# Score products that run 24 ahead of the transposed ones instead of 32, the first rows of maxima sent before the weights, and the first batch's key rows sent by ScalarE

## What is computed

```python
mod = silu(c) @ wmod                      # six vectors per batch: sa, ca, ga, sb, cb, gb
h = layernorm(x) * (1 + ca) + sa          # x is (4, 512, 256)
q, k, v = h @ wq.T, h @ wk.T, h @ wv.T    # 16 heads of 16
p = softmax(q @ k.T)                      # no scaling of the scores
x = x + ga' * ((p @ v) @ wo.T)            # ga', gb': sign kept, size at least 0.25
h = layernorm(x) * (1 + cb) + sb
r = softmax(h @ gate.T); top 4 of 32 experts, weights normalised
y = sigmoid(h @ sg) * shared(h) + sum over 4 experts of w_e * (silu(h@g_e) * (h@u_e)) @ d_e
x = x + gb' * y
```

## Time and profile before

| what | value |
|---|---|
| median of 3 runs | 648.5 us (648.0 to 648.52) |
| the profiled execution | 650.28 us |
| its span, first to last instruction | 648.5 us |
| TensorE busy | 584.2 us, 90% of the span |
| VectorE busy | 378.5 us, 58% |
| ScalarE busy | 261.3 us, 40% |
| GpSimd busy | 200.2 us, 31% |
| mean granted TensorE clock | 0.965 |

### The profile page before, as it was taken

The page is one execution under the profiler, slowest core; times in us unless marked ns, Lnnn a source line. Parts: engine busy times, 40 slices in busy tenths (PEclk is TensorE's granted clock), DMA queues, the critical chain, the costliest instruction groups (busy, mean ns, idle before and its releaser), DMA issues.

```text
span 648.5 us, 10653 instructions
## 1 busy us (share of the span) xinstructions
PE 584.2 (90%) x3118; PEld 320.4 (49%) x3119; DVE 378.5 (58%) x874; ACT 261.3 (40%) x523; POOL 200.2 (31%) x268
## 2 busy tenths in 40 slices
PE   4999999899998999989999998999889999999271
PEld 3453242234433344332433464565778889889251
DVE  6285757766769667696773665653534444444083
ACT  3214445654666646554456512001234344344100
POOL 6100000000000830007300480362256666666442
PEclk9957999999999999999999999999999999999797
DMA  6142161101401223012100127922455565552393
GB/s 210 37 129 86 34 198 28 30 2 41 83 8 28 90 85 82 6 30 83 50 1 2 41 83 322 266 101 66 121 147 147 156 170 155 163 161 53 107 410 131
DMA packets 41958, 67.17 MB, mean 104 GB/s; under 512 B 9099, under 2 KB 31764, under 8 KB 41564
## 3 DMA queue, kind: packets, MB, share of 16 engines
q1 hardware_dynamic: 29824, 45.62, 24.7%
q0 software_dynamic: 7680, 16.87, 7.5%
q10 hardware_dynamic: 4416, 4.20, 1.9%
HBM read 38.93 MB, written 27.51 MB: 102 GB/s over the span
## 4 chain that ended last, share of the span: by engine, by line
PE 73%; DVE 9%; DMA 5%; issue 4%; ACT 3%; POOL 3%; SPq 1%; POOLq 0%; ACTq 0%; DVEq 0%
PE ps L791 21%; PE ps L804 9%; PE ps L1017 8%; PE ps L1038 6%; PE ps L885 5%; PE ps L743 5%; PE ps L879 4%; DVE max_q L1121 3%; PE ps L1006 3%; PE ps L763 2%; DMA up_sb<-results 2%; PE ps L751 2%; PE ps L817 2%; POOL dispatched L457 2%; ACT probs L625 2%
## 5 line engine op out<-in xcount | busy, mean ns | idle before, releaser
L1121 DVE TENSOR_REDUCE max_q<-ps 128x1 f32<-128x512 f32 x256 | 163.2, 683 | 91.9 <-PE ps L763 90.8
L625 ACT ACTIVATE probs<-ps 128x512 f32<-128x512 f32 x256 | 138.2, 595 | 106.8 <-PE ps L791 106.7
L791 PE MATMUL ps<-q_rows,k_rows 32*128 32x512 f32 x512 | 153.7, 647 | 11.4 <-ACT probs L625 10.3
L763 PE MATMUL ps<-k_rows,q_rows 31*128 31x512 f32 x512 | 155.0, 687 | 0.3 <-DMA k_rows<-qk_raw 0.3
L475 POOL DMA_INDIRECT results<-y_sb,dest x96 | 94.5, 984 | 72.3 <-ACT y_sb L676 37.2
L791 PEld LDWEIGHTS ps<-q_rows,k_rows 32*128 32x128 f32 x512 | 49.0, 185 | 92.6 <-ACT probs L625 56.3
L1017 PE MATMUL ps<-up_sb,oT 128*128 x384 | 70.9, 328 | 1.3 <-issue 1.2
L804 PE MATMUL ps<-probs,v_ext 128*32 128x512 f32 x512 | 68.2, 605 | 0.0
L1017 PEld LDWEIGHTS ps<-up_sb,oT 128*128 128x128 f32 x384 | 61.3, 190 | 2.3 <-issue 2.2
L442 POOL TENSOR_TENSOR rstd<-veps,mhalf 128x4 f32<-128x4 f32 x4 | 4.1, 1037 | 167.4 <-DVE veps L1190 167.3
L763 PEld LDWEIGHTS ps<-k_rows,q_rows 31*128 31x128 f32 x512 | 48.7, 194 | 10.3 <-DVE max_q L1121 6.3
(11 more groups left out here) (172 smaller groups left out, 689.2 us busy)
## 6 DMA issues: line engine op xcount, KB each, us to landing
xe<-dispatched SPq DMA_DIRECT2D x96, 129.0 KB, 2.2
up_sb<-results SPq DMA_DIRECT2D x16, 512.0 KB, 8.5
up_sb<-in_up SPq DMA_DIRECT2D x2, 3072.0 KB, 14.8
dispatched<-pad_rows SPq DMA_DIRECT2D x33, 129.0 KB, 4.8
down_sb<-in_down SPq DMA_DIRECT2D x1, 3072.0 KB, 31.7
x<-in_x ACTq DMA_DIRECT2D x4, 512.0 KB, 5.2
q_rows<-qk_raw SPq DMA_DIRECT2D x64, 32.0 KB, 2.0
k_rows<-qk_raw SPq DMA_DIRECT2D x64, 32.0 KB, 2.0
```

What stands on the lines that cost most here:

```text
L625: act.activation(probs[:, u % 8, :], ps[:, st_bank(t.b, g, u), :], ACT.Exp).then_inc(exp_done, 1)
L763: pe.matmul(ps[:, banks[u % len(banks)], :], q_rows[32 * i:32 * i + ONE, b % 2, g, qt * P:(qt + 1) * P], k_rows[32 * i:32 * i + ONE, b % 2 ...
L791: pe.matmul(ps[:, st_bank(b, g, n), :], k_rows[32 * i:32 * i + 32, b % 2, g, kt * P:(kt + 1) * P], q_rows[32 * i:32 * i + 32, b % 2, g, :] ...
L1121: dve.tensor_reduce(max_q[:, g % 2, qt, i:i + 1], ps[:, banks[(16 * g + n) % len(banks)], :], AXX, ALU.max).then_inc(max_done, 1)
```

## The change

The lead is a number now, `LAG = 24`, and every place that had 32 or "two groups" goes by it. The lead-in does 8 score products of group 1 instead of 16. `turn_max` and `negate_max` move from u = 1 to u = 9, since the group's last maximum now exists eight steps later, and `ORDER` follows with the same entries in another order. In the last batch the steps by four begin at (2,8) instead of (2,0). In the lead-in the row of maxima is sent ahead of the loads of weights, and the keys' 16 DMAs are issued by ScalarE, between its copies. `place_rows` of later batches issues the same DMAs as before.

The number, the order of bank uses (first lines; the three other groups of the table move their `MAX` entry in the same way), the banks, and what is ahead of a step:

```diff
+LAG = 24
...
     ORDER = (
-        ("MAX0", "att"), ("TP0", "pre"), ("TP1", "pre"), ("QK0", "pre"), ("SG0@0", "fill"),
+        ("TP0", "pre"), ("TP1", "pre"), ("QK0", "pre"), ("SG0@0", "fill"), ("MAX0", "att"),
...
         def st_bank(b, g, n):
 
-            if b == B - 1 and g >= 2:
-                return (ST + SC)[(16 * (g - 2) + n) % 5]
+            alone = 16 * g + n - (16 * NG - LAG)
+            if b == B - 1 and alone >= 0:
+                return (ST + SC)[alone % 5]
             return ST[n % 2]
+
+        def ahead(b, g, n):
+
+            u = 16 * NG * b + 16 * g + n + LAG
+            return (u // (16 * NG), u // 16 % NG, u % 16) if u < 16 * NG * B else None
```

SyncE's queue in the lead-in (`projected` waits for ScalarE's copy, `place` issues the four DMAs of one group's queries or keys):

```diff
-            for half in range(2):
-                place_rows(lead, half)
+            projected(lead, 0)
+            place(lead, 0, 0)
+            place(lead, 0, 1)
+            projected(lead, 2)
+            place(lead, 0, 2)
+            place(lead, 0, 3)
+            max_rows(lead, 3)
             sp.dma_start(wmod[:, :, 2 * D:6 * D], wmod_in[:, 2 * D:6 * D].rearrange("(k p) n -> p k n", p=P)).then_inc(w_ld, 16)
             for w_d, w_s in ((wo, wo_sb), (gate, gate_sb)):
                 sp.dma_start(w_s[:, :, :], w_d.rearrange("(k p) n -> p k n", p=P)).then_inc(w_ld, 16)
-            max_rows(lead, 3)
```

ScalarE, in the turns and in the lead-in:

```diff
-                if u == 1 and (g < 3 or t.pre):
+                if u == 9 and (g < 3 or t.pre):
                     negate_max(t, g)
...
-            for c in range(4):
-                raw_qk(lead, c)
+            def key_rows(g):
+
+                c = 2 * (g // 2) + 1
+                written(act, lead, f"QK{c}")
+                for i in range(G):
+                    at = 32 * i + HD * (g % 2)
+                    act.dma_start(k_rows[32 * i:32 * i + HD, 0, g, :], qk_raw[at:at + HD, c, :]).then_inc(rows_ld[g], 16)
+
+            raw_qk(lead, 0)
+            raw_qk(lead, 1)
+            act.wait_ge(consts, 3)
+            key_rows(0)
+            raw_qk(lead, 2)
+            raw_qk(lead, 3)
+            key_rows(1)
             for m in range(2):
                 values_out(lead, m)
+            key_rows(2)
+            key_rows(3)
             negate_max(lead, 3)
```

TensorE; VectorE's `score_max` follows `ahead` and the shorter lead-in in the same way:

```diff
-                if u == 1 and (g < 3 or t.pre):
-                    turn_max(t, g)
                 if u in (5, 9, 13):
                     values(t.b, g, u // 4 - 1)
+                if u == 9 and (g < 3 or t.pre):
+                    turn_max(t, g)
...
                 for g in range(NG):
-                    step = 2 if g < 2 or t.pre else 4
-                    for u in range(0, 16, step):
+                    u = 0
+                    while u < 16:
+                        step = 2 if ahead(t.b, g, u) else 4
...
-            for n in range(16):
+            for n in range(LAG - 16):
                 score(0, 1, n, SC + ST)
 
-            pe.wait_ge(max_done, 32)
+            pe.wait_ge(max_done, LAG)
```

More of the change, by code:

```diff
@@ L297, in _, with row_buffer_free, projected, place @@
                 sp.dma_start(w_s[:, :, :], w_d.rearrange("(k p) n -> p k n", p=P)).then_inc(qkv_ld, 16)
+            def row_buffer_free(t, g):
+                n = t.b + 1
+                above(sp, st_full, 64 * (n - 2) + 16 * g + 16 if n >= 2 else 0)
+            def projected(t, c):
+                m, u = t.use(f"QK{c}")
+                sp.wait_ge(misc_free[m], u + 1)
+            def place(t, qk, g):
+                rows = (q_rows, k_rows)[qk]
+                for i in range(G):
+                    at = 32 * i + HD * (g % 2)
+                    sp.dma_start(rows[32 * i:32 * i + HD, (t.b + 1) % 2, g, :], qk_raw[at:at + HD, 2 * (g // 2) + qk, :]).then_inc(rows_ld[g], 16)
             def place_rows(t, half):
-                n = t.b + 1
                 for c in (2 * half, 2 * half + 1):
-                    m, u = t.use(f"QK{c}")
-                    sp.wait_ge(misc_free[m], u + 1)
+                    projected(t, c)
                 for g in (2 * half, 2 * half + 1):
[L308 to L312, removed]
+                    row_buffer_free(t, g)
+                    for qk in range(2):
+                        place(t, qk, g)
             def max_rows(t, g):
@@ L781, in scoreT @@
                     pe.wait_ge(maxrow, 16 * (NG * b + g) + 16)
-                if b == B - 1 and u >= 32:
-                    if u < 34:
+                alone = u - (16 * NG - LAG)
+                if b == B - 1 and alone >= 0:
+                    if alone < 2:
                         pe.wait_ge(exp_done, 64 * b + u - 1)
-                    elif u < 37:
+                    elif alone < 5:
                         pe.wait_ge(max_done, 64 * B)
@@ L938, in turn @@
                             for n in (u, u + 1):
-                                if g < 2:
-                                    score(t.b, g + 2, n)
-                                else:
-                                    score(t.b + 1, g - 2, n)
+                                score(*ahead(t.b, g, n))
                         for n in range(u, u + step):
                             between(t, g, n)
+                        u += step
             def finish(t):
@@ L1391, in turn @@
                     for u in range(16):
-                        if g < 2:
-                            score_max(t.b, g + 2, u)
-                        elif t.pre:
-                            score_max(t.b + 1, g - 2, u)
+                        if ahead(t.b, g, u):
+                            score_max(*ahead(t.b, g, u))
                         between(t, g, u)
```

4 lines of the change are left out of this document (2 added, 2 removed), and 2 rows, old and new, of the table ORDER.

## The result

| what | before | after |
|---|---|---|
| median | 648.51 us (645.54 to 651.3, 10 runs) | 654.05 us (649.58 to 655.58, 10 runs) |
| ratio | | 1.0078, 95% interval 1.0049 to 1.0106 |
| the profiled execution | 650.28 us | 653.47 us |
| its span | 648.5 us | 651.7 us |
| mean granted clock | 0.965 | 0.956 |

Slower by 0.8%, where I forecast no change and a range up to 651.0. Medians here are over all executions; ratios leave out executions that are over 1.5% longer than the fastest of their kernel. The page of the changed kernel shows the busy shares of before, and two digits of the granted clock are new: the seventh slice, 98 to 114 us, has 7 where before had 9, and the third from the end has 6 for 7.

What follows compares the result with a forecast made beforehand. VectorE was taken to bound the lead-in, and TensorE mostly the turns after it. The terms -4.83 + 0.35 + 0.17 + 1.59 + 1.5 + 1.2 sum to -0.02, so 648.5 us, range 645.4 to 651.0.

Steps and rivals of the forecast that it cites:

- Eight score products fewer: Lead-in: eight score products fewer at 0.603 us each of VectorE, -4.83 us.
- ScalarE's issues: Lead-in: key rows issued by ScalarE start the products for v 0.55 us late; first score product +0.35 us.
- First group: First group of the first turn: -0.36 us without the transposes, +0.53 for their return at u = 9, together +0.17.
- Transposes at u = 9: Three groups where VectorE bounded u = 1 and hid the transposes: 3 x 0.53 = +1.59 us; ends 0 and +8.
- The modulation's way through memory: First turn, (2,3): the broadcast lands at 104.0, VectorE wants it at 102.51, +1.5 us; ends 0 and +2.5.
- The last batch: Last batch: +0.36 us for group 2's first eight steps, more for the next four with the transposes, together +1.2.
- the small costs don't arise: Rival: VectorE has slack, transposes hide at u = 9, the broadcast lands in time; 645.4 us, chance 0.26.
- VectorE being behind at u = 9: Rival: TensorE stands at the transposes for VectorE's reduction of step 7; 651.1 us, chance 0.24.
- the clock's rival: Start of the first turn: TensorE's clock rises at another moment; 647.2 us if 3 us sooner, chance 0.08; could cost time.

Runs made afterwards that it cites:

- mod_first_again: The edit of mod_first (modulation sent ahead of group 1's row of maxima) on the changed kernel, run on another chip: 648.51 us, ratio 1.0001 to before.
- mod_first: The changed kernel with SyncE sending the modulation ahead of group 1's row of maxima in the first turn: ratio 1.0059 to before.
- best24: mod_first with group 0's keys sent by SyncE once copied, and ScalarE's issues behind its copies of v: 647.42 us, 0.9987; other chips 1.0025 and 0.995.
- keys_only: The kernel before, lead of 32 kept, with only the change's lead-in transfers (key rows from ScalarE's queue): ratio 1.0007.
- max_at_9: The kernel before, lead of 32 kept, with only the transposes of maxima and the negation moved to u = 9: ratio 1.0107.
- max_row_ahead: The kernel before, lead of 32 kept, with only the first rows of maxima put ahead of the weights' loads on SyncE's queue: ratio 1.0006.
- fill_wait: The changed kernel with a thrown-away product of two matmuls on TensorE where it would stand during the wait for the broadcast: ratio 1.0085 to before.
- after_again: The changed kernel unaltered, run again on a chip where before took 648.28 us: 650.84 us, ratio 1.0039.
- gate_late: The changed kernel with VectorE's four gate steps that need the broadcast put eight steps later: 650.39 us, ratio 1.0017 to before.
- warm: best24 with filler products behind the lead-in's score products and at its end, and the broadcast's first two uses one place later: 705.19 us.

## Why the prediction was wrong, step by step

1. *Eight score products fewer, -4.83*: right. VectorE's second block took 4.87 us (x8) for 9.65 (x16), -4.78.
2. *ScalarE's issues, +0.35*: the wait is as forecast (0.66 us for 0.55), but the first score product came at 27.33, 26.87, 28.20, 27.34, 27.98 and 26.84 us in six traces of this lead-in: the start of the stage moves by more than the term. -0.37 in the profiled one.
3. *First group, +0.17*: -0.36 of it should have stood between the first transposed product and (0,5); measured +1.43 (9.18 us for 7.75), since the clock came back at 55.5, 9.3 us after the turn's start, against 6.1. At 1.8 us over the forecast this is the second largest miss. Six traces with this lead-in gave 9.18 four times, 8.23 and 7.96. The same program gives 8.0 and 9.2 (mod_first_again and mod_first), so part of it is chance; best24's three gave 8.54, 8.26 and 8.29. In all of them the distance follows the moment at which the clock comes back, counted from the first transposed product: 4.8 us gives 7.28 (keys_only), 6.1 gives 7.75 (before), 6.5 gives 7.96, 7.8 gives 8.54 (best24), 9.3 gives 9.18. None with the lead of 24 reached before's 7.75. On the mean of the nine traces with the lead of 24 against the four with 32 (before, keys_only, max_at_9, max_row_ahead), the turn starts 4.7 us sooner but the clock is back only 2.9 sooner, and the distance is 8.70 for 7.86. The two groups overlap, so this share of the term is likely and not shown. I had the clock as a rival, with the gain named first and the loss in half a sentence.
4. *Transposes at u = 9, +1.59*: right in kind and size. In mod_first_again, free of the wait, the offset goes from -4.28 at (0,5) to -2.49 at the end of batch 2: +1.79, for the +2.12 of this term and the transposes of term 3.
5. ***The modulation's way through memory, +1.5*: this is the step that failed.** The chain was right within 0.6 us in every link (queue free at 89.4 and landing at 104.0, less the 3.7 us by which the kernel is early there, for 85.97 and 100.86), and the wait was 1.75 us. Its price was not: 4.58 us more than mod_first's over the same eight steps, and 4.21 in the pair of runs on one chip. By fill_wait, one trace, 2.5 of it is the stand and 2.0 is the clock, which fell to 1.2 GHz behind a stand of 1.76 us and stayed there for 6.8 us. My upper end for it, +2.5, was the wait with nothing behind it.
6. *The last batch, +1.2*: undersized. After goes from +2.66 to +4.44, +1.78; mod_first_again from -2.49 to -0.71, the same. The steps by four begin later: (2,5) to (2,9) takes 5.12 us for 3.90, with score products and the logits in it. And the next four steps, with the transposes, take 5.26 for 4.35.

Together: -3.72 at (0,5), +0.09, +5.82 over the eight steps (4.58 of it the wait and the clock, the other 1.24 as in mod_first), +0.47, +1.78, and -1.3 in the experts, which the change doesn't touch: +3.2 of span. That last part is no property of the change: after_again has -0.2 there, mod_first_again -1.4, gate_late -1.8. The size of the miss is not stable either: after_again's 650.84 lies inside my range, 2.6 us over before where the first measurement had 5.5.

*The rivals.* That the small costs don't arise fell at (2,3). VectorE being behind at u = 9 gave the side but not the cause: TensorE never stood at its transposes in the turns. In the clock's rival I took the row of 1.22 us (x2) for a pair of products; it is one, and the 43% stand. The Trainium skill's page "TensorE: Matmul & The Clock Gate" (Part 1) says that the array's speed follows how busy it has been. fill_wait agrees (filled, the clock stays; unfilled, it falls); warm, at 1.2 GHz for 28 us of unbroken work, does not, and the fall of gate_late and mod_first in batch 1 is not in mod_first_again.

## What to carry to other kernels

Where a step of a hand-written order is moved, follow what stands behind it on every queue: here the move of a tiny row of maxima by eight steps held up a 1.5 MB broadcast, and putting the two in the other order on SyncE's queue gave back 4.2 us between two profiled executions on one chip and 2.3 us of the median. Price a stand of TensorE such as the ones here, of 1.2 and 1.8 us, as more than its length, since the low clock may follow it, and give that case its own share of the range. Before a lead is changed, look for a placement that depends on it modulo something: `(n + 2) % G` is right for multiples of four alone.

## What the runs showed of the hardware that I had not expected

- The granted clock fell to half behind a stand of 1.76 us (and, in after_again, of 1.20), stayed at 1.0 in max_at_9, where VectorE waited 0.61, and fell in warm at 52.7 us with no gap at all. One program gives a fall in one run and none in the next (mod_first and mod_first_again at 198 us).
- The broadcast of 1.5 MB took 10.9 to 12.5 us to land from one kernel to the other, so a wait worked out to the microsecond carries 1.6 us of doubt from it alone.
- Two transposed and two score products take 1.07 us on different pairs of row strips and 1.92 on the same.
- A full-array product among those on strips costs more than its own time: one score product took 1.05 us between fillers at 2.4 GHz, where four in a row take 1.14 at the start of best24's lead-in (27.39, x8).
